# Quantised rows split into f16 halves on GpSimd, q and k normed there, narrow score blocks in one exp, and a refitted order

## What is computed

```
x = x + 0.5 * ffn(layernorm(x), w_gate, w_up, w_down)
x = x + attn(layernorm(x), Wq, Wk, Wv, Wproj, ...)
x = x + 0.5 * ffn(layernorm(x), w_gate, w_up, w_down)

def fp4_quant_dequant(x):            # blocks of 16 along the row
    scale = max(max(abs(block)) / 6, 1e-12)
    q = nearest of (0, .5, 1, 1.5, 2, 3, 4, 6) to abs(block / scale), with the sign, * scale
def fp4_linear(x, w): return fp4_quant_dequant(x) @ fp4_quant_dequant(w).T
ffn:  h = silu(fp4_linear(x, w_gate)) * fp4_linear(x, w_up);  fp4_linear(h, w_down)   # 704 hidden columns
attn: q, k = rotary(rmsnorm(heads of x @ W.T))       # 16 heads of 16 columns each
      causal softmax(q k / 4); 8 pairs of heads, out = (a1 - lam * a2) @ v, layernorm per head, @ Wproj.T
```

## Time and profile before

| | us |
|---|---|
| median of 3 runs | 2098.32 (2097.1 to 2098.84) |
| the profiled execution's own time | 2095.44 |
| its span, first to last instruction | 2093.4 |
| busy: PE | 1858.8 (89%) |
| busy: ACT | 1697.5 (81%) |
| busy: DVE | 1550.4 (74%) |
| busy: POOL | 1371.6 (66%) |
| first exp starts, last exp starts | 205.7, 2000.1 |

### The profile page before, as it was taken

How to read it: one execution, slowest core, us unless ns; L and a number is a source line. 1 busy time by engine, 2 the same in 40 slices (tenths; PEclk the granted TensorE clock), 3 DMA queues, 4 the chain that set the end, 5 groups by cost and what they waited for, 6 DMA issues and landing times. The chain is left out here.

```text
span 2093.4 us, 36773 instructions
## 1 busy us (share of the span) xinstructions
PE 1858.8 (89%) x13634; PEld 783.9 (37%) x13634; DVE 1550.4 (74%) x3324; ACT 1697.5 (81%) x2467; POOL 1371.6 (66%) x1439
## 2 busy tenths in 40 slices
PE   2687999999998999999999898999999898999966
PEld 1343343343433444344432343444433333432223
DVE  7889988686656898787945988888855778741275
ACT  3455988979988898878989888888899799889942
POOL 7788886665645786777854876876854657640155
PEclk9899999999999999999999999999999999999987
DMA  4134444334222445243421445333341344220013
GB/s 129 31 61 88 84 82 79 58 65 81 46 49 43 77 80 100 59 83 59 74 59 21 82 77 92 88 72 54 58 87 32 69 71 82 61 49 1 11 35 72
DMA packets 477474, 135.99 MB, mean 65 GB/s; under 512 B 458224, under 2 KB 477040, under 8 KB 477296
## 3 DMA queue, kind: packets, MB, share of 16 engines
q1 hardware_dynamic: 477296, 133.65, 33.9%
HBM read 11.96 MB, written 8.39 MB: 10 GB/s over the span
## 5 line engine op out<-in xcount | busy, mean ns | idle before, releaser
L1072 ACT ACTIVATE probs<-psum 128x1024 f32<-128x1024 f32 (+3 forms) x1280 | 1069.4, 938 | 71.4 <-PE psum L1357 55.1
L1375 PE MATMUL psum_o<-probs,v_sb 128*32 128x512 f32 (+3 forms) x5120 | 568.0, 539 | 16.4 <-POOL probs L977 11.6
L1320 PE MATMUL psum<-w_gu_T,xT 128*128 128x512 f16 (+1 forms) x2304 | 506.6, 369 | 44.1 <-DVE hq L1154 14.7
L1357 PE MATMUL psum<-q_stack,k_stack 64*128 64x512 f16 (+3 forms) x2560 | 381.7, 351 | 77.4 <-ACT probs L1072 58.1
L1320 PEld LDWEIGHTS psum<-w_gu_T,xT 128*128 128x128 f16 x2304 | 214.4, 99 | 308.7 <-issue 44.1
L977 POOL TENSOR_SCALAR_AFFINE_SELECT probs<-probs 128x512 f32<-128x512 f32 x256 | 179.3, 707 | 196.3 <-ACT probs L1072 195.7
L1333 PE MATMUL psum<-w_down_T,hT 128*128 128x256 f16 x2176 | 265.9, 278 | 32.0 <-DMA hT<-h 15.7
L1357 PEld LDWEIGHTS psum<-q_stack,k_stack 64*128 64x128 f16 x2560 | 98.5, 93 | 487.9 <-ACT probs L1072 355.2
L945 POOL TENSOR_TENSOR hq<-grid,qscale 128x704 f32<-128x704 f32 x128 | 184.3, 1441 | 97.1 <-DVE grid L1171 97.1
L1333 PEld LDWEIGHTS psum<-w_down_T,hT 128*128 128x128 f16 x2176 | 210.1, 99 | 94.1 <-issue 27.1
L952 POOL TENSOR_TENSOR h<-hq,h 128x704 f16<-128x704 f32 x128 | 200.1, 1564 | 61.9 <-ACT h L1028 61.4
(11 more groups left out here) (120 smaller groups left out, 2348.6 us busy)
## 6 DMA issues: line engine op xcount, KB each, us to landing
xb<-L_attn_x SPq DMA_DIRECT2D x16, 512.0 KB, 4.1
out<-xb SPq DMA_DIRECT2D x16, 512.0 KB, 3.3
xT<-x SPq DMA_TRANSPOSE x128, 3.1
hT<-h SPq DMA_TRANSPOSE x128, 3.5
k_stack<-st SPq DMA_TRANSPOSE x64, 3.3
q_stack<-st SPq DMA_TRANSPOSE x64, 3.3
k_stack<-L_ffn_w_down SPq DMA_DIRECT2D x1, 704.0 KB, 4.0
k_stack<-L_ffn_w_gate SPq DMA_DIRECT2D x1, 512.0 KB, 5.6
```

The costliest lines, as they stand in the source:

```text
L1072: nc.scalar.activation(probs[:, s % 3, 2 * u:2 * u + 2, q0:CHUNK], psum[:, plan.pairs[s, u]:plan.pairs[s, u] + 2, q0:CHUNK], ACT.Exp, scal ...
L1320: last = nc.tensor.matmul(bank(e)[:, 0:hi - lo], xs[:, x, t % 2, k, :], w_gu_T[:, w, k, lo:hi], start=n == 0, stop=n == len(parts) - 1)
L1357: last = nc.tensor.matmul(psum[:, plan.pairs[s, u] + j, q0:CHUNK], k_stack[half, at, h, kt % NTC * P:(kt % NTC + 1) * P], q_stack[half, c ...
L1375: last = nc.tensor.matmul(psum_o[at:at + VD, q0:CHUNK], v_sb[:, kt // NTC % SLOTS * NTC + kt % NTC, 2 * g + u, :], probs[:, s % 3, 2 * u + ...
```

## The change

1. In passes 0 and 3 the stages dequant are gone, and the high half moves from ACT to POOL. block_scales now splits the scale itself into two parts: high has so few bits that a grid point times it is exact in f16, low is the rest. POOL makes both halves, points x high part and points x low part, each by half_of. Points are written over the quotients (hq) instead of over the squares, and the ring of squares GU goes from 2 to 1. block_scales has three more DVE instructions on 32 or 44 columns (192 times), and keeps its PSUM bank until the last of them.
2. norm_qk is the same multiplication, on POOL.
3. The steps with q0 of 256 or 384 (128 of 640) have one part: the scores of both heads lie side by side in one pair of banks and are taken by one exp. The number of matmuls stays.
4. COST, DUE and WIDE are refitted, so the order of all engines changes.

Counted over the program, ACT has 320 instructions fewer (192 high halves and 128 exps), DVE 512 more (576 small ones, less 64), and POOL 64 more.

```diff
-    "high_h0": (42390, 2000650, -2232219, -3797522, -613153, -230570, 2653919, 2875932, 635974, 2547059, -3291457, -862265, -3047681, -586356, -2517900, -472010, 739771, -2249008, 3824028, 4341813, 2582720, 2668532, 2165188, 1971905, 1720841, 2519055, 883311, 1018537, 2262926, 3574454, 1269271, 2507284),
...
-GU = 2
+GU = 1
...
-        add(("grid_" + kind, *u), "vector", at("grid_" + kind), [("square_" + kind, *u)])
-        add(("points_" + kind, *u), "vector", at("points_" + kind), [("grid_" + kind, *u)], [],
-            [place] if kind == "x" else [])
-        add(("dequant_" + kind, *u), "gpsimd", at("dequant_" + kind), [("points_" + kind, *u)], [], [place] if kind == "h" else [])
-        add(("high_" + kind, *u), "scalar", at("high_" + kind), [("dequant_" + kind, *u)], [(half, key)])
-        add(("low_" + kind, *u), "gpsimd", at("low_" + kind), [("high_" + kind, *u)], [], [(own, key)])
+        add(("grid_" + kind, *u), "vector", at("grid_" + kind), [sq])
+        add(points, "vector", at("points_" + kind), [("grid_" + kind, *u)], [], [place])
+        weight = HALVES_X if kind == "x" else None
+        add(("high_" + kind, *u), "gpsimd", at("high_" + kind), [points], [(half, key)], weight=weight)
+        add(("low_" + kind, *u), "gpsimd", at("low_" + kind), [("high_" + kind, *u)], [],
+            [(own, key)], weight=weight)
...
-            add(("norm_qk", t), "vector", at("norm_qk"), [("rms", c), ("rope_add", t), before("norm_qk")])
+            add(("norm_qk", t), "gpsimd", at("norm_qk"), [("rms", c), ("rope_add", t), before("norm_qk")])
...
+def in_parts(s):
+
+    return 1 if STEPS[s][4] >= CHUNK // 2 else 2
...
+        def half_of(kind, key, n):
+
+            scale = scales(kind, key)[:, n, :]
+            return nc.gpsimd.tensor_tensor(
+                by_block(halves(kind, key)[:, n, :]), by_block(buffers(kind, key)[0]),
+                scale.unsqueeze(2).broadcast_to([P, scale.shape[1], QB]), ALU.mult)
...
                         before = user["gu"][GU_OF[e[1:]] - GU]
-                        if turn["dequant_" + before[0], *before] > turn["divide_h", *e[1:]]:
-                            until(act, "act", quantised, DEQUANT["dequant_" + before[0], *before] + 1)
+                        until(act, "act", points_ready, POINTS["points_h", *before] + 1)
...
+                    to, at, n = probs[:, s % 3, :, q0:CHUNK], plan.pairs[s, u], in_parts(s)
+                    if n == 2:
+                        to, src = to[:, 2 * u:2 * u + 2, :], psum[:, at:at + 2, q0:CHUNK]
+                    else:
+                        to = to.rearrange("p (u j) q -> p j u q", j=2)
+                        src = psum[:, at:at + 2, 0:2 * (CHUNK - q0)].rearrange("p j (u q) -> p j u q", u=2)
...
-                nc.vector.tensor_scalar(q, am, SCALE_UP / 6.0, floor, ALU.mult, ALU.min).then_inc(read(e)[0], 1)
-                until(dve, "dve", *read(e))
-                nc.vector.reciprocal(r, q).then_inc(scales_ready, 1)
+                wait(done(nc.vector.tensor_scalar(q, am, SCALE_UP / 6.0, floor, ALU.mult, ALU.min)))
+                nc.vector.reciprocal(rscale[:, i, 0:nb], q).then_inc(scales_ready, 1)
+                wait(done(nc.vector.tensor_scalar(high, q, HALF_STEP + 1.0, None, ALU.mult)))
+                wait(done(nc.vector.scalar_tensor_tensor(high, q, -HALF_STEP, high, ALU.mult, ALU.add)))
+                nc.vector.tensor_tensor(low, q, high, ALU.subtract).then_inc(read(e)[0], 1)
```

More of the change, by code:

```diff
@@ L520, in whole_plan @@
             add(("turn_qk", t), "sync", at("turn_qk"),
-                [("low_qk", t), before("turn_qk"), ("scores", steps_of(steps, c - 2)[-1], 1) if c >= 2 else None,
-                 ("scores", held, 1) if c >= SLOTS else None],
+                [("low_qk", t), before("turn_qk"), last_part("scores", steps_of(steps, c - 2)[-1]) if c >= 2 else None,
+                 last_part("scores", held) if c >= SLOTS else None],
                 [], [("st", t)], lands=TURNED_QK)
@@ L785, in buffers, with scales @@
             return hq[:, i, :], XU + i, I // QB
+        def scales(kind, key):
+            i, nb = buffers(kind, key)[1:]
+            return qscale[:, i, :, 0:nb]
         def squares(kind, key):
             return bank(("square_x", "x", *key))[:, 0:2 * C] if kind == "x" else grid[:, GU_OF[kind, *key] % GU, :]
[L791 to L793 removed]
         def halves(kind, key):
@@ L944, in gpsimd_stages @@
                         until(pool, "pool", points_ready, POINTS["points_h", *e[1:]] + 1)
[L945 to L947 removed]
+                    before = before_in(ring(kind, key, 1), key)
+                    if before:
+                        until(pool, "pool", *landed(kind, before))
+                    half_of(kind, key, 0)
                 elif e[0] in ("low_x", "low_h"):
                     kind, key = e[1], e[2:]
[L950 to L953 removed]
+                    if kind == "x" and key[0] in (1, 2):
+                        until(pool, "pool", high_ready, HIGH["high_x", *e[1:]] + 1)
+                        high, low = (halves(kind, key)[:, i, :] for i in range(2))
+                        nc.gpsimd.tensor_tensor(low, buffers(kind, key)[0], high, ALU.subtract)\
+                            .then_inc(low_ready, 1)
+                    else:
+                        half_of(kind, key, 1).then_inc(low_ready, 1)
                 elif e[0] == "rope_add":
@@ L958, in gpsimd_stages @@
                         .then_inc(roped_ready, 1)
+                elif e[0] == "norm_qk":
+                    t = e[1]
+                    i = t % NTC
+                    until(pool, "pool", *read(("rms", t // NTC)))
+                    until(pool, "pool", roped_ready, t + 1)
+                    nc.gpsimd.tensor_tensor(
+                        roped[:, i, :].rearrange("p (h d) -> p h d", d=HD),
+                        roped[:, i, :].rearrange("p (h d) -> p h d", d=HD),
+                        qk_rstd[:, i, :].unsqueeze(2).broadcast_to([P, 4 * NH, HD]), ALU.mult)\
+                        .then_inc(qk_n_ready, 1)
                 elif e[0] == "low_qk":
@@ L1096, in block_scales @@
             def block_scales(e, src, i, nb, floor):
-                am, q, r = mine(e)[:, 0:nb], qscale[:, i, 0:nb], rscale[:, i, 0:nb]
+                am, q = (mine(e)[:, n * nb:(n + 1) * nb] for n in range(2))
+                high, low = (scales(e[1], e[2:])[:, n, :] for n in range(2))
                 nc.vector.tensor_reduce(am, by_block(src), AX_X, ALU.max, apply_absolute_value=True)\
```

185 lines of the change are left out of this document (85 added, 100 removed), and 131 rows, old and new, of the table DUE.

## The result

| | median us | runs | against the kernel before |
|---|---|---|---|
| before | 2097.71 | 2096.93 to 2098.84 | |
| changed | 2078.03 | 2075.84 to 2080.57 | 0.9906, interval 0.9889 to 0.9923 |

Faster by 19.7 us, where 49 were forecast. The profiled execution of the changed kernel took 2080.57 us, the longest of its four; against the 2095.44 of before it shows 14.9 us of those 19.7.

A forecast was written before the change was run, and what follows sets the result against it. Exps on ACT were taken to pace attention in nearly half of the parts and PE the rest; -65 + 24 - 5 - 3 = -49 took the profiled 2095.4 to 2046, forecast 2049 us (-2.3%), range 2015 to 2106.

The forecast's parts named there:

- By the share above 0.44 x 148 = -65.: ACT between first and last exps: 148 us saved, counted at the 44% of score weight loads that waited for an exp.
- exps pace half: Attention: the forecast's own case, exps pace nearly half of the parts, PE the rest; range 2028 to 2080, chance 0.52.
- 172.7 us off ACT: ACT: time saved by high halves of h (102.9) and x (41.9) leaving and by joint exps (15.0 and 12.9).
- DVE +24: DVE's dense feed-forward stretches: 42% of the 58 us that DVE gains net from small instructions and departing norms is charged.
- The bank of a scale is held 0.6 us longer, with 7 banks: 0.: PSUM bank of block_scales: holding it 0.6 us longer, with 7 banks, was taken to cost 0.
- POOL 0, joint exps 0 on top, GU 0: POOL's added work, the joint exps' extra stride and wait for both heads, and the single squares tile: each charged 0.
- Opening -5, end -3: Before the first exp: moved tiles -16, small instructions +10, norms +1, giving -5 us; final tile chain: three links, -3 us.
- PE takes all: PE's hidden slack in attention steps: ACT's gain nearer 0.7 x 148 = 104 us, total -88, 2010 us; chance 0.15.
- the port: DVE's grids and points wait for two POOL products instead of one: +65 us on DVE, half on path, 2082; chance 0.07.
- PE as the bound: PE: only 58 us of open idle behind exps can be had, half taken; total -13, 2085 us; chance 0.12.
- it doesn't do what it says: POOL and ACT: f16 products at 1.564 us, joint exps save nothing; ACT -145, POOL +90, 2070 us; chance 0.03.
- The slower case: DVE paces the dense stretches, small instructions costing time from about 97% busy: +12, 2110 us, or +50, 2148; chance 0.11.

## Why the prediction was wrong

The direction was right, and 2078 us lies inside the stated range, but the size was not: -19.7 us instead of -49. One term carries the miss.

- **"By the share above 0.44 x 148 = -65."** This step failed: the case "exps pace half" took the share of weight loads that waited for an exp as the price of ACT's time. The share was a count of waits. The runs give 0.16 (taken out before), 0.19 (added after) and 0.12 (in bulk). With 0.175, the middle of the first two, the booked 148 us are worth 26, not 65.
- **172.7 us off ACT.** Busy time fell by 119.1. The sum took each instruction at its row's mean, but an ACT instruction that follows another starts before the first one's record ends: the exp of 1.063 us comes every 0.925 us, an overlap of 0.14. A removed instruction between others frees its spacing, not its record. Count times mean, summed over ACT's rows, fell by 209 us (1987.7 to 1778.5), more than was booked; but what the records overlap fell from 290 to 200 us, and that is what is missing. An estimate of 0.14 for each of 320 instructions gives 44 of these 90 us; the rest may be that ACT has more gaps now. The Trainium skill, Perfetto Trace Analysis, "Optimizing Scalar/DVE Operations", says that the part of an instruction that waits for the acknowledgement of its writes overlaps with the next one; the trace agrees that they overlap, by 0.14 us, and does not show in what. With the 94 us that left the middle the term is 94 x 0.175 = -16.
- **DVE +24.** That the split alone cost 24.0, by the run without it, is luck: the term was 0.42 x 58 for split and norms together, in the dense stretches, and measured were 0.26 x 91.7 for the split. DVE gained 35 us instead of 58 (split 103 instead of 115, points 0.12 us shorter each), and its dense stretches did not fill (651 to 647 us).
- **"The bank of a scale is held 0.6 us longer, with 7 banks: 0."** Wrong: the waits for it went from 21.5 to 37.1 us in the first row alone, and fall to 7.8 without the split.
- **POOL 0, joint exps 0 on top, GU 0.** Nothing that can be measured, as far as they were tried: POOL's norms and its wait for the one h16 tile, the joint exps, the one tile of squares. POOL gained 23 us, not 58. But the joint exps' own 28 us of ACT were 8.
- **Opening -5, end -3.** -12.5 and +3.9. That together they are the 8 us forecast is luck, since each is off by about 7, the other way. The split's 10 us in the opening were right (9 by the run without it); what the moved tiles gave was put too low. Why the end is longer is open.
- **Rivals.** "PE takes all" fell with the price of ACT. Three rivals gave times within 8 us of 2078: the port (2082), PE as the bound (2085), and "it doesn't do what it says" (2070). PE as the bound looks right, with PE at 94% and ACT at 82%, nearly the sign that the prediction named for it; but fewer matmuls of the hidden product gave nothing before and 0.17 a microsecond after, so PE's work there was no bound. The 2070 case has one half right: joint exps save little; but a half of h takes 1.433 us, not 1.564. Its 2070 doesn't follow from its terms: 0.44 x 0.86 x 145 is 55, and -55 + 24 - 8 gives 2059. The port rival falls: DVE's grid and points of h, 1.148 and 1.203 us before, take 1.199 and 1.079, less together, though two products follow each other on POOL. The rule of the Trainium skill, SBUF — State Buffer, "Who interferes with whom", says that such instructions contend while both run, and is not refuted by this: in both kernels they take from 0.83 us to over 2. What fell is the prediction's step from it, that two products in a row double the excess. The slower case did not come: dense stretches stayed at 88% on DVE, and no run tried the 97% that it starts from. Its price was real, though: work added to DVE cost 0.91 and 0.97 a microsecond, and with the old due times the changed kernel is 155.6 us slower than the one before. The prediction credited the new order with the opening alone; in neither run without a refit is there a gain. Whether DVE is what makes the order with the old due times slow is not shown.

A ledger with the measured prices: ACT -16, DVE 0.26 x 35 = +9, opening -12.5, end +3.9, together -16, where the profiled spans differ by -14.6. It is a check of the size and no proof: the prices hold for the whole span, and 0.26 is that of the split, not of the norms that left DVE. With the split's own 24.0 us, less the 9 that are in the opening, it would be -10. Still open is why the kernel before gained nothing from fewer matmuls and the changed one 9.7 us, and how DVE's price of 0.9 for more divides between bank and queue.

## What to carry to other kernels

Where four engines run fixed lists and the chain changes engine all the time, don't price a saving by the engine's busy share or by how many waits it ends; take a little of its work away, or add some, and measure. How much of the chain lies on the engine is a first guess and no more: ACT had 15% of the chain in 76% of busy time, 0.2 a microsecond, and was worth 0.12 to 0.19; DVE 24% in 76%, 0.3, for 0.26; but PE 26% in 89%, 0.3, for 0.17, and POOL 16% in 67%, 0.24, for 0.03. Price added work apart from saved work where it holds a bank: three small instructions more cost three to four times what three fewer gave. Due times fitted to one set of stages don't serve another: with the old ones the changed kernel ran 155.6 us over the kernel before, and the new ones made the kernel before 99.0 us slower.

## What the hardware showed unexpectedly

- Back to back, ACT's records overlap by 0.14 us (1.063 us long, 0.925 apart), so sums of rows overstate its busy time.
- PE at 89% of the span, nine tenths in most slices, was no bound: 57 us fewer of it in the hidden product gave 0 (1.0007, 0.9996 to 1.0018). The Trainium skill, Perfetto Trace Analysis, "Identifying the Most-Contended Engine", says to improve the engine with the highest occupancy first, and that for matmuls busy time is a poor measure, in whose place it names the share of peak work and the weight loads' busy share. The second half held here; the loads have 37% before. The first leads to ACT at 81%, and a microsecond of it was worth 0.16.
- DVE's small instructions on 44 columns cost 0.141 us (constants, PSUM to SBUF) and 0.204 (with a second tensor), against 0.264 for the one with a column operand.
- Three such instructions more, 192 times, cost 87 us, and three fewer gave 24.
